# Attention on one core: a rewritten order of one head's work on five engines, other units computed whole, and a wait moved to the first score

## The reference, cut to what matters

```python
q, k, v = (proj(Wq, bq), proj(Wk, bk), proj(Wv, bv))          # [b, 16, 2048, 32]
scores = jnp.einsum('bhqd,bhkd->bhqk', q, k) / jnp.sqrt(jnp.float32(HD))
scores = scores + bias                                        # a slope per head times the key's place
scores = jnp.where(causal, scores, jnp.finfo(scores.dtype).min)
attn = jax.nn.softmax(scores, axis=-1)
ctx = jnp.einsum('bhqk,bhkd->bhqd', attn, v)
# then ctx @ Wo + bo, plus the experts (top 2 of 8) on the same normed rows, plus x
```

## Time and profile before

| what | us |
|---|---|
| median of 3 runs | 1968.61 (1963.74 to 1979.11) |
| the profiled execution, first to last instruction | 1970.9 |
| head 0 starts, about | 336.8 |
| head 31 starts, about | 1442.8 |
| last value product of head 31, about | 1488 |
| TensorE busy | 1897.6 (96%) |
| VectorE, ScalarE, GpSimd busy | 1501.2, 1400.8, 1372.3 |

### The profile page before, as it was taken

One profiled execution on the slowest core, in us unless ns is written; L12 is line 12 of the kernel. 1 busy time (PEld: TensorE's weight loads), 2 busy tenths in 40 slices (PEclk: granted clock), 3 DMA queues, 4 the chain that ended last, 5 costly groups with the idle time before them and its releaser, 6 DMA issues. The chain is left out here.

```text
span 1970.9 us, 39142 instructions
## 1 busy us (share of the span) xinstructions
PE 1897.6 (96%) x8656; PEld 1425.0 (72%) x8657; DVE 1501.2 (76%) x3466; ACT 1400.8 (71%) x2728; POOL 1372.3 (70%) x1183
## 2 busy tenths in 40 slices
PE   6999999999999999999999999999998989999997
PEld 5787777676767777777677776776756767887876
DVE  6454566888989989899899898898966965666654
ACT  4333322998999989999999899998973335555554
POOL 4111113898988989889889898898948846666664
PEclk9999999999999999999999999999999999999998
DMA  8577758242242432423324224243226766656554
GB/s 268 193 260 258 272 179 283 75 114 64 73 104 61 97 80 63 113 62 81 96 62 108 69 71 106 61 96 81 62 72 183 252 197 118 104 103 104 104 99 66
DMA packets 119241, 242.13 MB, mean 123 GB/s; under 512 B 17632, under 2 KB 54368, under 8 KB 112896
## 3 DMA queue, kind: packets, MB, share of 16 engines
q1 hardware_dynamic: 101120, 205.84, 36.0%
q0 software_dynamic: 18080, 35.81, 10.3%
HBM read 139.28 MB, written 104.21 MB: 124 GB/s over the span
## 5 line engine op out<-in xcount | busy, mean ns | idle before, releaser
L1173 POOL TENSOR_TENSOR probs_lo<-probs,probs_hi 128x512 fp32r<-128x512 f32 x781 | 984.1, 1291 | 158.6 <-ACT probs L1208 156.7
L1207 ACT ACTIVATE probs_hi<-s_ps 128x512 fp32r<-128x512 f32 x905 | 602.0, 665 | 84.3 <-DVE s_ps L1280 80.2
L1208 ACT ACTIVATE probs<-s_ps 128x512 f32<-128x512 f32 x964 | 613.3, 670 | 9.8 <-DVE s_ps L1280 6.4
L1259 DVE TENSOR_REDUCE m_part<-m_ps 128x1 f32<-128x512 f32 x744 | 491.1, 685 | 9.5 <-PE m_ps L1500 5.9
L1516 PE MATMUL s_ps<-q_st,k_st 100*128 100x512 f32 (+3 forms) x880 | 327.9, 413 | 16.5 <-ACT probs L1208 11.8
L1500 PE MATMUL m_ps<-k_st,q_st 98*128 98x512 f32 (+2 forms) x840 | 282.0, 377 | 0.3 <-DVE m_part L1256 0.3
L1535 PE MATMUL o_ps<-probs_hi,v_split 128*96 128x512 f32 (+3 forms) x720 | 266.8, 380 | 1.7 <-POOL probs_lo L1173 1.7
L1536 PE MATMUL o_ps<-probs_lo,v_split 128*96 128x512 f32 (+3 forms) x720 | 259.2, 363 | 0.0
L1256 DVE CUSTOM_DVE_ANT_0 m_ps<-m_ps,mask_row 128x128 f32<-128x128 f32 x496 | 242.0, 498 | 22.5 <-PE m_ps L1500 16.3
L1516 PEld LDWEIGHTS s_ps<-q_st,k_st 100*128 100x128 f32 x880 | 161.5, 190 | 103.0 <-ACT probs L1208 37.9
L621 POOL TENSOR_TENSOR v_rows<-v_raw,v_rows 128x512 fp32r<-128x512 f32 x32 | 41.2, 1291 | 229.4 <-ACT v_rows L677 229.4
(11 more groups left out here) (236 smaller groups left out, 3658.2 us busy)
## 6 DMA issues: line engine op xcount, KB each, us to landing
v_d<-v_rows SPq DMA_DIRECT2D x7, 3072.0 KB, 9.4
v_split<-v_d SPq DMA_DIRECT2D x22, 768.0 KB, 8.5
k_st<-k_hi_d SPq DMA_DIRECT2D x44, 256.0 KB
q_st<-q_hi_d SPq DMA_DIRECT2D x44, 256.0 KB
xn_d<-xs SPq DMA_DIRECT2D x8, 1024.0 KB, 11.7
q_hi_d<-qk_hi SPq DMA_DIRECT2D x32, 256.0 KB, 8.0
q_lo_d<-qk_lo SPq DMA_DIRECT2D x32, 256.0 KB, 7.9
k_hi_d<-qk_hi SPq DMA_DIRECT2D x32, 256.0 KB, 3.5
```

The source lines that it names most:

```text
L1173: nc.gpsimd.tensor_tensor(*low_operands(u), ALU.subtract).then_inc(lo_ready_pool, 1)
L1207: nc.scalar.activation(probs_hi[:, P_SLOT[u]], scores, ACT.Exp, scale=SCALE)
L1208: nc.scalar.activation(scores if kind == "Q" else probs[:, P_SLOT[u]], scores, ACT.Exp, scale=SCALE).then_inc(p_ready, 1)
L1259: V.tensor_reduce(top, scores, AX.X, ALU.max).then_inc(m_taken, 1)
```

## The change

The strings `KIND`, `ORDER` and the table `BACK` are replaced. The counts of all letters stay: 34 S, 40 M, 34 V, 25 P, 5 W and 4 Q units. Whole units are now 4, 9, 12, 18 and 31 (before: 2, 9, 18, 26, 29); VectorE's units are 7, 21, 25 and 29 (before: 14, 21, 23, 30). Six value products and three low parts are carried over (before: eight and four). The bank of each unit and the ring of weights are as before. On TensorE the wait for `m_placed` moves from the head's start to the first score, and the wait for `st_loaded` to the first maxima unit.

```diff
-KIND = "PPWPPPPPPWPPPPQPPPWPPQPQPPWPPWQPPP"
+KIND = "PPPPWPPQPWPPWPPPPPWPPQPPPQPPPQPWPP"
-ORDER = ("SMMMVVVMVMMVLSSMVMLLSMVMMVOVSLMSMVSLSMLMLVSMSMVSLMLMLVMMOVSMSSVMMSVMVMDOSLMVLLSVSMVSVMSMVSMMVSMVMSLD"
-         "LVSLMLLVMDLSMVSMMSSVMSVLSVXWVSLVLLDSOVSVLLS")
-BACK = {'V': 8, 'L': 4, 'O': 1}
+ORDER = ("LLLVMMVLLMVSSSLMMVMSMMVVVMMOMLSSSVSLLMVSMLLDMVOSMLVVVSSLLVMVMSMMSSMVMMO"
+         "VSSVMSMSVMVMSSLLLLMMLSMLLVVMMSVVSDMMMSSMVMVDSSMMVVSMMSLLLXVVVWDOSSLVVSVS")
+BACK = {'L': 3, 'V': 6, 'O': 1}
@@ step_n of TensorE
-                pe.wait_ge(m_placed, 32 * (n + 1))
-                if maxima:
-                    pe.wait_ge(st_loaded[r1], 16 * ST_DMAS * st_round)
                 for kind, u, back in ATTEND if maxima else LAST_ATTEND:
+                    if (kind, u) == ("S", 0):
+                        pe.wait_ge(m_placed, 32 * (n + 1))
+                    if maxima and (kind, u) == ("M", 0):
+                        pe.wait_ge(st_loaded[r1], 16 * ST_DMAS * st_round)
```

## The result

The kernel after runs in 1959.05 us (median of 11 runs, 1955.39 to 2011.28) against 1971.54 us of the kernel before (11 runs beside it); the ratio is 0.9941, 95% interval 0.9927 to 0.9954. That is 0.6% or some 12 us faster, where 30.6 us had been forecast. The profiled execution has a span of 1957.1 us against 1970.9.

What follows compares the result with a forecast made beforehand. TensorE bounds the kernel, at 35.64 us a head over a 34.25 floor. A head of 34.7 saves 28.2 over 30 heads, plus 1.8 at heads 0 and 1 and 0.6 at head 31: 30.6 us, giving 1938.0, range 1926 to 1955.

Steps and rivals of the forecast that it cites:

- the clock: Rival: one pause per head, say at S0 behind the rows, lowers the granted clock, giving 2017 us; chance 0.03.
- The floor of 34.25: PE's time for one head priced by matmul starts without waits, 34.25 us, unchanged by the new order.
- The stall at unit 33: Head's last score, waiting for ACT to free unit 31's bank: late by 0.05 us instead of 0.65.
- the loop's turn: At the turn of PE's loop, 0.3 us in every third head, charged as 0.1 a head.
- The wait for the placed rows: Moved from head's start to S0: rows land at 3.5 us, PE comes at 4.34, so cost 0.
- Head 1's start: Head 0 and head 1's start: rows' wait partly covered, unit 33's stall gone, earlier maxima; 1.8 us gained.
- Head 31: Last head: new S0 wait of 0.95 us lies inside the wait for unit 33's bank; 0.6 us saved.
- the small waits of the new order: Waits inside each head: only the chain's largest lateness counts, 0.3 us, plus 0.05 for five other places.
- my list of tight places: Units 7, 8, 18, 24 and maximum M28, each with under 0.1 us in hand; 0.05 charged for all.
- The chain named as the tightest: DVE's rows and low part, unit 32, then ACT's exponentials free unit 33's bank; next head's S1 about 0.3 us late.
- the second rival: Nearly the floor: overlapping DVE instructions shorten its chain, 34.35 us a head, 1927.5 us in all; chance 0.13.
- the waiting moves instead of going: Rival: dearer hand-overs stall some eight tight places, the head keeps 0.9 of its 1.39 us, 1952 us; chance 0.18.

Runs made afterwards that it cites:

- e10: Kernel after with the head's order laid out anew so releases come at least 0.15 us early where possible; 1934.86 us, ratio 0.9826 to the kernel before.
- e1: Kernel after with both TensorE waits, placed rows and operands, put back at the head's start; period 36.15 against 35.36, total 1986.43 us.
- e3: Kernel before with exponentials and low parts at half width in heads 1 to 31; period 35.38 against 35.64, total of 2013.5 us not used.
- e5: Kernel after with one maximum, M38, moved ahead of unit 28's scores; period 35.353 against 35.357, total 1952.22 us.
- e7: Kernel after with maximum 3 moved between units 0 and 1; period 35.079 against 35.357, total 1945.92 us.
- e9: Kernel after with three moves together: unit 18 behind V12, maximum 3 between units 0 and 1, earlier chunk sums with maximum 10 moved; 1942.9 us, ratio 0.9854.
- e6: Kernel after with unit 18's scores moved behind the product V12; period 35.263 against 35.357, total 1956.17 us.

## Why the prediction was wrong in size

By its own steps:

- **What bounds the kernel: right; the clock: nearly.** PE sets the time, and the granted clock is 1.00 from 407 us to head 30's end, before and after. In head 31 of the kernel after it fell to 0.50 from 1466.8 to 1470.2 us, behind a pause of 1.67 us. The floor of 34.25 is borne out from above: single heads of e10 take 34.4.
- **The stall at unit 33: right.** Forecast late by 0.05 instead of 0.65; measured in time, with 0.19 in hand. The 0.08 left there is the loop's turn, forecast 0.1.
- **The wait for the placed rows: right, and the part that carries the change.** Cover replaced by the move; e1 and e3 show both halves. The rows land 3.47 after the transposition, worked out as 3.5.
- **Head 1's start: wrong.** Head 1's first score comes 1.7 us earlier than before, which looks like the forecast 1.8, but 1.6 of it had been there before head 0 began. From the transposition before head 0 the change gave 0.2. From head 0's own transposition to the score it is 4.46 instead of 5.70, 1.2 less, of about the size foreseen; but that transposition comes 1.0 later than in the old order, and the forecast had no term for head 0 getting longer.
- **Head 31: the number came out by luck**, 0.8 for 0.6. From head 30's last score to the last value product pass 45.18 us, 3.4 of them at the clock of 0.50. In e5, e7 and e9, which have the same order in head 31 and keep the clock at 1.00 there, it is 43.5 to 43.6, so the change is worth some 2.4. PE's pause and the stretch around it, kernel after:

```profile
1465.90 0.47 PE L1535 MATMUL o_ps<-probs_hi,v_split 128*96 128x512 f32 x1 [1.67 <-POOL probs_lo L1173]
```

```profile
1464.00:1474.00 10.00, 8.33 (x25) 4.75 (x25) 2.97 (x5) 6.66 (x12) 7.95 (x7) 0.83 0.03 7
```

  The same pause of 1.65 us stands in the kernel before at 1479.6 and in e9 at 1454.8, and there the clock stayed at 1.00. At the start of head 31 unit 0 did wait for the rows and it lay inside, as said:

```profile
1431.03 0.45 PE L1516 MATMUL s_ps<-q_st,k_st 100*128 100x128 f32 x2
1432.07 0.49 PE L1516 MATMUL s_ps<-q_st,k_st 100*128 100x512 f32 x1 [0.59 <-DMA q_st<-m_rows]
...
1433.44 0.56 PE L1516 MATMUL s_ps<-q_st,k_st 100*128 100x128 f32 x2
```

  2.41 us pass between the scores 33 and 1 (forecast 2.6, before 3.62).
- **The step that failed: the small waits of the new order.** The prediction had "Latenesses in one chain do not add; the largest counts: 0.3 a head" and charged 0.05 for five further places together, the loop's turn 0.1. Measured is 1.1 for the 0.45. Two things were wrong in it. The term for a hand-over was mis-sized: I counted the release as free when the other engine's record ended, or 0.05 behind it, and it takes 0.15 in hand to cost nothing. What was missing is the 0.10 in the step behind. So "under 0.1 in hand" is a loss of 0.05 to 0.15 at each place, and places with 0.1 to 0.15, which I did not list, cost too. Two of the dearest, maximum 7 and V2, were not on my list of tight places at all, with 0.02 and 0.01 in hand; which duration on my clock misplaced them is open. And the sentence on chains is true of one chain (e5) but was applied to the whole head, which has several: e6 to e9 show that their losses add to nine tenths.
- **The chain named as the tightest was not the dearest.** Unit 1 of the next head was to be 0.3 late and lose that; it is in time (0.01 in hand) and loses 0.15. VectorE's records overlap a little: the low part of unit 29 starts at 1005.12, before the rows' record ends at 1005.19, and ends 1.60 after the transposition instead of 1.7. That is the argument of the second rival, and it held for this chain. Unit 32 loses 0.18, and unit 18, maximum 7 and V2 0.13 or 0.14 each. Three maxima (7, 28, 34), of which I had put one among the tight places, take 0.23 together; unit 8, which I had listed too, has 0.24 in hand and loses nothing.
- **The rival** "the waiting moves instead of going" described what happened: it kept 0.9 of the 1.39 and gave 1952; measured are 1.1 kept and 1959. Its argument against, that the old order's small waits lay behind ScalarE's backlog, was the same error: its losses of 0.02 to 0.07 at six places with 0.09 to 0.14 in hand were the 0.15 showing itself, and should have raised its chance and its price.

## What to carry to other kernels

When an order is planned by hand against an engine that is nearly full, give each hand-over its own price: by these traces a waiting TensorE instruction needs the releaser's record to end 0.15 us ahead, and losses in chains that have slack between them add. Look first in the old trace for small losses that the plan says should not be there; they tell the missing term. And read a part of a forecast from an anchor next to the change: two parts of this one seemed right only because the stage before ended earlier and because the clock fell. And before a stall is taken out, ask which later wait it covers, and move that wait with it, as here, where the order alone would have cost 0.5 us a head instead of winning 0.3.

## What the runs showed of the hardware that I had not expected

- A wait below some 0.2 us leaves no idle time in the record. A release that comes with 0.11 to 0.13 in hand shows only in the step behind the waiting instruction (units 7 and 24: 0.05 and 0.03), one with 0.00 to 0.03 in hand shows in the step before it too (unit 18: 0.02 and 0.10). The recorded duration of the waiting instruction is longer, 0.47 to 0.50 instead of 0.39 for V2 and unit 32. PE is busy for 995.00 of 995 us in the kernel after with 1.1 of each 35.4 us lost, and for this in e10, which is 1.8% faster a head:

```profile
420.00:1415.00 995.00, 994.87 (x4621) 741.24 (x4620) 902.65 (x2205) 954.10 (x1925) 905.42 (x719) 1.00 0.34 84
```

  The Trainium skill (Perfetto Trace Analysis, Identifying the Most-Contended Engine) says that matmul busy time is a poor metric for how close a kernel is to its limit; these traces agree. What follows the speed is the count of matmuls in an equal stretch: 4495, 4530, 4621, which is 0.8% and then 2.0% more, beside periods shorter by 0.8% and 1.8%.
- The release of a bank by ScalarE and by VectorE costs the same 0.15 us, whichever matmul waits: a score (unit 18 behind ScalarE 0.13 with 0.03 in hand, unit 32 behind VectorE 0.18 with -0.02), a maximum (7: 0.14 with 0.02) or a value product (V2: 0.13 with 0.01).
